# Graph layer with attention and expert adapter on one core: tail order, last group of the counts, and mask moved between engines

## What is computed

```
xn = layernorm(x)                                  # x: 1250 nodes x 768
x  = x + gnn(xn, src, dst) + linear_attention(xn)  # 20000 edges, 3 graph attention layers of 4 heads
x  = x + adapter(layernorm(x))

gat_conv: e = leaky_relu(as[src] + ad[dst]); p = exp(e - max per dst)
          out[dst] = sum(p * h[src]) / sum(p)      # per head
attention: q, k = elu + 1; y = q (k^T v) / (q sum(k)); times W_proj
adapter:  h = gelu(x @ Wd.T); per token the best of 4 experts by softmax(h @ Wg.T)
          h = h + weight * (h @ We[best].T + be[best])   # not for the first 5 tokens
          return (h @ Wu.T) * gamma
```

## Time and profile before

| | |
|---|---|
| median of 3 runs | 1424.25 us (1423.36 to 1425.78) |
| the profiled execution, its own time | 1424.32 us |
| its span in the profile | 1422.3 us |
| TensorE busy | 1355.7 us (95%) |
| VectorE busy | 1055.7 us (74%) |
| ScalarE busy | 490.5 us (34%) |
| GpSimd busy | 47.5 us (3%) |
| mean granted TensorE clock | 0.989 of full |

### The profile page before, as it was taken

How to read it: one execution, slowest core, us unless ns; L and a number is a source line. 1 busy time by engine, 2 the same in 40 slices (tenths; PEclk the granted TensorE clock), 3 DMA queues, 4 the chain that set the end, 5 groups by cost and what they waited for, 6 DMA issues and landing times.

```text
span 1422.3 us, 21073 instructions
## 1 busy us (share of the span) xinstructions
PE 1355.7 (95%) x8144; PEld 1266.5 (89%) x8144; DVE 1055.7 (74%) x1932; ACT 490.5 (34%) x812; POOL 47.5 (3%) x44
## 2 busy tenths in 40 slices
PE   5998999999999899999999999999999999999886
PEld 4964566999999799899999999999999999999774
DVE  6867998699999752686776677676757766778666
ACT  3210123233443521444333433343243334323372
POOL 3102000000000050000000000000000000000000
PEclk9999999999999899999999999999999999999998
DMA  9310000212221484611101110111012011105003
GB/s 278 116 68 2 0 1 0 88 70 88 79 79 55 147 239 136 171 37 35 41 1 70 36 40 1 70 39 38 4 67 76 1 70 37 42 1 142 1 1 109
DMA packets 23619, 91.59 MB, mean 64 GB/s; under 512 B 3681, under 2 KB 4864, under 8 KB 20589
## 3 DMA queue, kind: packets, MB, share of 16 engines
q1 hardware_dynamic: 22609, 88.07, 19.3%
q10 hardware_dynamic: 924, 2.30, 0.6%
HBM read 79.30 MB, written 11.06 MB: 64 GB/s over the span
## 4 chain that ended last, share of the span: by engine, by line
PE 52%; DVE 7%; ACT 1%; issue 1%; DVEq 0%
PE psum L1686 25%; PE psum L101 8%; PE psum L102 8%; PE psum L103 8%; DVE hN L1313 1%; PE psum L1700 1%; DVE prob L1297 1%; DVE prob L1291 1%; PE psum L1740 1%; DVE acc L1335 0%; DVE x1l L1320 0%; DVE acc L1351 0%; PE psum L1755 0%; ACT prob L1517 0%; DVE xll L1326 0%
## 5 line engine op out<-in xcount | busy, mean ns | idle before, releaser
L1686 PE MATMUL psum<-hN,prob 125*125 125x193 f32 x2400 | 409.0, 327 | 1.5 <-DVE hN L1313 1.5
L1686 PEld LDWEIGHTS psum<-hN,prob 125*125 125x125 f32 x2400 | 395.3, 187 | 2.0 <-issue 1.8
L1517 ACT ACTIVATE prob<-prob,acol 125x1250 f32<-125x1250 f32 x120 | 161.2, 1343 | 381.4 <-DVE prob L1291 381.4
L1297 DVE SCALAR_TENSOR_TENSOR prob<-prob,cnt 125x1250 f32<-125x1250 f32 x120 | 174.7, 1456 | 56.4 <-ACT prob L1517 56.4
L1291 DVE SCALAR_TENSOR_TENSOR prob<-vrow,ncol,urow 125x1250 f32<-125x1250 f32 x120 | 182.0, 1517 | 9.5 <-PE psum L1686 9.5
L734 DVE CUSTOM_DVE_ANT_0 junk<-mask,arow 125x1250 bf16<-125x1250 uint8 x120 | 174.8, 1457 | 3.1
L101 PE MATMUL psum<-woh,xlh 128*125 128x384 f32 x360 | 127.4, 354 | 2.6 <-DVE acc L1335 2.6
L102 PE MATMUL psum<-wol,xlh 128*125 128x384 f32 x360 | 123.0, 342 | 0.0
L101 PE MATMUL psum<-wph,x1h 128*125 128x384 f32 x330 | 117.8, 357 | 4.8 <-PEq L949 1.9
L103 PE MATMUL psum<-woh,xll 128*125 128x384 f32 x360 | 122.2, 340 | 0.0
L619 PE MATMUL psum<-hot_src,hot_dst 125*125 125x418 bf16 x540 | 110.8, 355 | 3.2 <-DVE hot_src L433 2.9
(11 more groups left out here) (236 smaller groups left out, 2218.8 us busy)
## 6 DMA issues: line engine op xcount, KB each, us to landing
arow<-scratch_a SPq DMA_DIRECT2D x12, 625.0 KB, 4.1
urow<-scratch_uv SPq DMA_DIRECT2D x12, 625.0 KB, 4.1
vrow<-scratch_uv SPq DMA_DIRECT2D x12, 625.0 KB, 5.7
wq_raw<-in_w_qkv SPq DMA_DIRECT2D x6, 1152.0 KB, 6.8
wp_raw<-in_w_pair SPq DMA_DIRECT2D x6, 1152.0 KB, 7.5
wo_raw<-in_w_out SPq DMA_DIRECT2D x6, 1152.0 KB, 5.2
wl<-in_w_gat SPq DMA_DIRECT2D x4, 1152.0 KB, 11.3
xN<-in_x SPq DMA_DIRECT2D x10, 336.0 KB
```

Of the source, the lines that this page charges most:

```text
L1297: nc.vector.scalar_tensor_tensor(prob[n % RING][:, :], prob[n % RING][:, :], 1.0, cnt[:, n % NT, :], op0=ALU.min, op1=ALU.mult).then_inc(p ...
L1517: nc.scalar.activation(prob[n % RING][:, :], prob[n % RING][:, :], ACT.Exp, bias=acol[:, n // NT, n % NT:n % NT + 1]).then_inc(e_ready, 1)
L1686: last = nc.tensor.matmul(bank(t // 2)[0:P, 193 * (t % 2):193 * (t % 2) + 193], ring[:, t * P:(t + 1) * P], hN[i % 2][:, j, 193 * s:193 * ...
```

## The change

It does four things. The subtraction of the minima goes from GpSimd to ScalarE, as an addition of minus_low, which VectorE makes. The mask of each group is made by ScalarE with Sign, at the start of the next group's step, before the turned counts. The last group's three transposed batches go to banks 0, 1 and 2 with no wait for a free bank, and VectorE copies them to cnt. TensorE waits for ones_col just before the first product of keys and values. In the adapter's tail the steps stand in another order on the three engines, and ScalarE has a small Exp of its own (exp_first) ahead of weigh_experts(2).

```diff
             own.done(nc.gpsimd.tensor_scalar(ncol[:, :, :], acol[:, :, :], SLOPE - 1.0, None, ALU.mult))
-            pool.wait_ge(a_low, 1)
-            nc.gpsimd.tensor_scalar(abT[0:HEADS, :], abT[0:HEADS, :], low[:, :], None, ALU.subtract).then_inc(a_low, 1)
...
-            def has_edge(w):
-                dve.wait_ge(ct_ready, 3 * (w + 1))
-                nc.vector.tensor_scalar(mask[:, w, :], ct[w % 2][:, :], 1.0, None, ALU.min).then_inc(mask_ready, 1)
...
-            nc.vector.tensor_reduce(low[:, :], abT[0:HEADS, :], axis=AX.X, op=ALU.min).then_inc(a_low, 1)
+            own.done(nc.vector.tensor_reduce(low[:, :], abT[0:HEADS, :], axis=AX.X, op=ALU.min))
+            nc.vector.tensor_scalar(minus_low[:, :], low[:, :], -1.0, None, ALU.mult).then_inc(a_low, 1)
...
-                if w:
-                    has_edge(w - 1)
...
-            has_edge(NT - 1)
+            dve.wait_ge(ct_ready, 3 * NT)
+            nc.vector.tensor_scalar(mask[:, NT - 1, :], ct[(NT - 1) % 2][:, :], 1.0, None, ALU.min).then_inc(mask_ready, 1)
+            for k, (_, t0, n) in enumerate(TURNS):
+                dve.wait_ge(turn_full, len(TURNS) * (NT - 1) + k + 1)
+                nc.vector.tensor_copy(cnt[:, t0:t0 + n, (NT - 1) * P:NT * P],
+                                      bank(k)[0:P, 0:P * n].rearrange("p (t n) -> p t n", t=n)).then_inc(turn_free, 1)
...
+            act.wait_ge(a_low, 1)
+            nc.scalar.activation(abT[0:HEADS, :], abT[0:HEADS, :], ACT.Identity, bias=minus_low[:, :]).then_inc(a_low, 1)
             act.wait_ge(wq_in, 16)
...
+            def has_edge(w):
+                act.wait_ge(ct_ready, 3 * (w + 1))
+                nc.scalar.activation(mask[:, w, :], ct[w % 2][:, :], ACT.Sign).then_inc(mask_ready, 1)
+
             for w in range(NT):
+                if w:
+                    has_edge(w - 1)
                 if 0 < w < NT - 1:
                     take_turned(w - 1)
...
             take_turned(NT - 2)
-            take_turned(NT - 1)
...
-                    if len(TURNS) * w + k >= 2:
+                    if w == NT - 1:
+                        at_bank = k
+                    elif len(TURNS) * w + k >= 2:
                         pe.wait_ge(turn_free, len(TURNS) * w + (0, -1, 1)[k])
...
                 if i:
                     pe.wait_ge(kvb_ready, i)
+                else:
+                    pe.wait_ge(ones_col, 1)
...
-            pe.wait_ge(ones_col, 1)
...
             add_choice(1)
-            add_up(0, 6)
+            add_up(0, 3)
             full_low(1)
-            add_up(6, 10)
+            add_up(3, 4)
             choose(2)
-            add_up(10, 12)
+            add_up(4, 5)
             combine(2)
+            add_up(5, 7)
             add_choice(2)
+            add_up(7, 8)
             full_low(2)
-            add_up(12, 20)
+            add_up(8, 20)
...
             deviation(NT - 1)
-            full_high(1)
             gelu(3)
             take_x2(NT - 1)
+            full_high(1)
             take_routes(6, 8)
             gelu(4)
             take_routes(8, 10)
+            nc.scalar.activation(exp_first[:, :], eps[:, :], ACT.Exp)
             weigh_experts(2)
...
             up(2, 3)
-            up(3, 6)
             routes(6, 8)
             down(4)
-            up(6, 9)
+            up(3, 4)
             routes(8, 10)
-            up(9, 12)
+            up(4, 8)
             turn_choice(2)
-            up(12, 20)
+            up(8, 20)
```

More of the change, by code:

```diff
@@ L211, in front @@
         ends = sb("ends", [HALF, 2, 2])
+        minus_low = sb("minus_low", [HEADS, 1])
         start_i, start = sb("start_i", [NT, 1], I32), sb("start", [NT, 2])
@@ L1184, in convolutions @@
         order = sb("order", [P, 1, EX])
+        exp_first = at("exp_first", 10272, [P, 1])
         res_in = [sem(f"res2_in{i}") for i in range(2)]
```

## The result

The changed kernel takes **1416.59 us** (median of 22 runs, 1412.99 to 1434.29) against 1424.40 us of the kernel before (median of 22, 1422.41 to 1427.91). The ratio is 0.9942, with a 95% interval of 0.9936 to 0.9948: faster by 0.58%, some 8.3 us of 1424.4; the medians differ by 7.8 (the run at 1434.29 was in a slower state and is not in the ratio). The profiled execution took 1416.86 us, its span is 1414.9; of the kernel before they were 1424.32 and 1422.3.

What follows compares the result with a forecast made beforehand. VectorE was taken to pace the count stage, TensorE the group borders, and serial chains the counts' end and the tail. Terms -2.85, -0.7, -1.13, -2.1, -1.85 sum to -8.63, from 1424.25 to 1415.6 us; range 1412.8 to 1419.5.

Steps and rivals of the forecast that it cites:

- all terms, clock up: Likeliest case: every edit gives its booked gain and TensorE's clock stays high at the first keys; 1415.6 us, chance 0.52.
- rival (1): Before attention, TensorE's clock falls as in the old kernel; 1417.7 us, chance 0.26.
- subtraction off GpSimd, with minus_low: Start of counts: VectorE's 3.05 us stall goes, the small multiply costs 0.2 us; net -2.85 us.
- masks: Group borders: VectorE sheds 0.81 us ten times, but it becomes idle time while waiting for TensorE; booked at nothing.
- last group's counts: End of count stage: transposes no longer wait for bank 6 and VectorE makes the copies; -0.7 us, bounds 0.2 and 1.0.
- ones_col: Start of attention: TensorE's first keys matmul no longer waits for GpSimd's memset; -1.13 us.
- clock at the first keys: TensorE at 2.4 GHz instead of 1.2 GHz at attention's start; -2.1 us taken, bounds 0 and -2.7.
- tail: Adapter's end: earlier choice, partly eaten by six tiles of stores; -1.85 us, bounds -0.5 and -2.95.
- Lost: 3.05 us: Count stage: hot_src at 124.93 would have begun at 121.88 without GpSimd's operation, and this comes back whole.
- rival (5): Group borders: ScalarE's step with Sign no longer fits, TensorE waits nine times; 1431.5 us at a 6.0 us step, chance 0.04.
- 2.95 us: Adapter's tail: the turned choice comes this much earlier, at 1406.1 instead of 1409.06.
- Rival (2): The tail gives nothing: twelve ups at low clock and six tiles of stores eat the earlier choice; 1417.5 us, chance 0.08.

Runs made afterwards that it cites:

- both experiments with GpSimd: Changed kernel with the minima's subtraction back on GpSimd: 1419.77 us; the same plus a second GpSimd pass adding 0.0: 1422.41 us.
- old tail: Changed kernel with the adapter's tail in its earlier order on three engines and without the early small Exp: 1419.12 us.
- ten matmuls: Changed kernel with ten idle 128 x 384 matmuls on TensorE between up 7 and the turned choice, into a bank nothing reads: 1416.52 us.
- the sign change: Changed kernel with minus_low made by ScalarE, leaving VectorE only the reduction: 1416.45 us.
- last group: Changed kernel with the final group's turned counts in two alternating banks again, all copied by ScalarE: 1417.88 us.
- two passes: Changed kernel with the minima subtracted on GpSimd, followed there by an addition of 0.0 to the same tile: 1422.41 us.
- all together: Changed kernel with minus_low made by ScalarE, ten idle matmuls in the tail and idle matmuls at both stage borders: 1415.42 us (five runs).

## Why the prediction was right

The time came out 1.0 us above that of the likeliest case, but the case itself, "all terms, clock up", did not: the clock of 0.50 in the first keys, the prediction's own sign for rival (1), was there, for half as long as before. In the profiled execution the kernel's span became 7.4 us shorter where the sum said 8.63, term by term:

| term | predicted | measured | by |
|---|---|---|---|
| subtraction off GpSimd, with minus_low | -2.85 | -2.72 | the loop's stretch; both experiments with GpSimd |
| masks | 0 | 0 | 126.44 against 126.30 |
| last group's counts | -0.7 | -0.73 | 5.79 against 5.06 |
| ones_col | -1.13 | -1.11 | 1.14 and 1.15 against 0.04 |
| clock at the first keys | -2.1 | -1.12 | 16.58 against 15.46 |
| tail | -1.85 | -2.22 | 28.20 against 25.98 |
| outside the terms | 0 | +0.50 | the first, sixth to ninth stretch of the table |

Part of the closeness is luck. The clock's term was 0.98 us too large and the tail's 0.37 too small; and among the stretches that no edit touches, +1.55 us at the last block's start happened to meet -1.56 behind the heads.

**GpSimd.** The step "Lost: 3.05 us" held (2.72 + 0.41 is 3.13), and that the operation is the cause is shown by doing it once and twice. The term's second part was mis-sized: 0.2 for minus_low, measured 0.41. The row that I took, 0.16 for a small chained operation, priced the instruction; the idle time of 0.25 that the chain puts ahead of the next operation was left out.

**Masks.** Booked at nothing, and worth nothing, for the reason given: VectorE's idle time at the borders doubled from 5.8 to 11.3 us and the borders stayed 7.08 us apart. The prediction counted ten masks moved where it is nine, which changes nothing in a term of 0. ScalarE's Sign took 1.25 us (1.34 by the exp row), without a table load: rival (5) needed 5.2. The Trainium skill (ScalarE: Activation LUTs, Rules for kernel authors) would have these masks on VectorE. The measured price is 1.25 us against 0.81, so the rule is right on cost, and the cost lands on an engine with 2.96 us to spare.

**Last group and ones_col.** Both terms came out within 0.03 us. Both were read as one serial chain, in which nothing else could be late next.

**The clock.** This is the step that failed, though inside its bounds. "I take -2.1, nearer to the end where it stays up": in the profiled execution it fell, for some 3 us of work instead of 5.6, and gave 1.12. It is not a matter of yes or no for this kernel: from first keys to third k feature it was 14.08 to 14.11 us in five profiles (subtraction on GpSimd once and twice, masks, old tail, ten matmuls) and 15.43 to 15.52 in three (the changed kernel, without the early Exp, the sign change), and the code next to this border is the same in all eight but for the masks. What picks the one or the other is open. Against 16.58 the two are worth 2.5 and 1.1 us; 2.1 is near the mean of the eight (2.0), but no single execution gives it, and 16.58 itself is from the one profile of the kernel before. Rival (1), that it falls exactly as before, came nearest to true in the kernel that still had the wait for ones_col (16.36).

**What the sum had no term for.** The clock has other places of this kind: the start of the counts (1.2 us, in three profiles), the last block's start (+1.55 here: 0.57 at 553 to 557), the residual behind the heads (-1.56: in the kernel before the clock is 0.80 and 0.77 in the means of 1326 to 1330 and 1330 to 1334, in the changed one 1.00), and 1372 to 1375 (+0.64: 0.54, where the kernel before has 1.00 from 1370 to 1382). The first score of the last block came 8.7 us behind the block's start in four profiles (before, ones_col, last group, two passes) and 10.2 to 10.3 in seven; what picks the one or the other is open. Together they can make two profiles of nearly the same code differ by 2 or 3 us, and so I set the stretches side by side and not the spans. Between the start of attention and the last block nothing was lost: the stretch from the third k feature to the last block's first memset is 289.82 us before and 290.07 after (289.02 to 290.90 in all thirteen profiles).

**The tail.** "2.95 us" for the turned choice was 3.45. By the rows, the first routes matmuls stand 2.34 us behind std (expected 1396.44 - 1394.10 = 2.34), but choose(2) 6.54 us, not 6.9, and esum 8.16, not 8.65; from esum to the turned choice it is 3.35 us in both kernels. So the second batch of routes was sized 0.4 too late. The term for the end, 14.3 us from the turned choice, was 14.47, and it was the stores as reckoned: six tiles in about 8.6 us (the window of the ten matmuls' run), 1.4 us a tile. Rival (2) had the right mechanism, and it took 1.23 of the 3.45 us, not all.

## What to carry to other kernels

A GpSimd operation beside a paced VectorE is charged to VectorE: look for the one long instruction among equal ones, and move the GpSimd work to an engine with idle time even if it costs a small operation more. Price an edit in its own stage, by whose wait ends last there: the masks' 7.3 us of VectorE time (9 x 0.81) bought nothing, while one misplaced wait of TensorE for GpSimd's memsets cost 1.1 us by itself, and in its profile 0.9 more by the clock. Before a small gain is put down to an edit, see how far profiles that share the code differ in that stretch: for the tail's end here it is 0.7 us. And in a tail that ends in stores, count the tiles that are still to be written behind the last dependency: that sets how much of an earlier start is kept.

## What the runs showed of the hardware

- One GpSimd pass over 12 x 1250 f32 held a VectorE instruction of 0.25 us for 3.44 us, and a second pass the next one for 3.38; the hot_src between them took 0.82 instead of 0.54.
- GpSimd's ncol, 125 x 120 and untouched by every edit, took 0.79 us in the eight profiles in which VectorE does the small multiply (the changed kernel among them) and 2.50 to 2.52 us in the five in which it doesn't (before, the subtraction on GpSimd once and twice, the sign change on ScalarE, all together). VectorE runs the same instructions beside it in both; what sets it, and whether it cost anything, is open.
- A table load doesn't wait for the activation's input: without the early Exp it begins at 1395.17, 0.02 us behind the end of the last copy of the routes, while its Exp's input is begun at 1395.39. It takes 1.28 us, and the Exp begins 0.01 us behind it. Sign ran nine times among the Copies with no load between 100 and 246 us.
- The granted clock fell behind 3 us in which TensorE had nothing to do (0.58 at 124 to 128, with the subtraction on GpSimd; the kernel before had the same gap without a fall), and it stayed at 1.00 at the two stage borders in both kernels that filled them with matmuls, at the first of which it did so in five of eight others too. With ten matmuls in the tail's gap it fell all the same: 1.00 up to 1402, 0.50 from 1404 to 1406. Filling matmuls can also cost: the seven ahead of the barrier delayed it by 0.23 us.
- The profiles show low stretches at five places outside the tail that differ between executions. That they, and nothing else, make the spread of the runs was not tried.
